# Two attention layers on one core: transposing and scaling the first half of the output inside the attention stage

## Chip, cores and metric

The kernel runs on one core of a Trainium2 chip. The metric is the device time of one execution in microseconds (us). PE is TensorE, DVE is VectorE, ACT is ScalarE, POOL is GpSimd and SP is SyncE, which here only issues DMAs.

## What is computed

The input is 1024 tokens of width 512. Four blocks follow each other, each with a residual and a layer norm: causal attention with 32 heads of width 16 and an adapter, a lookup feed-forward, causal attention with 32 query heads on 8 key/value heads, and a SwiGLU feed-forward. The change lies where an attention ends and its output projection begins:

```python
attn = jax.nn.softmax(scores, axis=-1)
y = jnp.einsum('bhqk,bhkd->bhqd', attn, v)
...
y = y + jnp.einsum('bhqk,xhkd->bhqd', ascores, av)     # first layer only
y = y.transpose(0, 2, 1, 3).reshape(B, T, C)
return jnp.einsum('btc,oc->bto', y, w_proj)
...
x = _layernorm(x + attention(x), axis=-1)
```

## The kernel before

The kernel is a series of stages. A stage is a block in which each engine runs its own list of instructions in order, held back only by semaphores, and all engines meet at its end. Two functions matter here, and each runs once for each layer.

`attention` works through 16 units. A unit is one group of four heads (`g`, eight groups) and one half of the tokens (`c`, 512 queries), in the order g0c0, g0c1, g1c0, and so on, so unit 15, the last, is a long one (c = 1, eight key tiles) and unit 14 is the last of the first token half. For each key tile PE makes the scores (L880), ACT takes their exponential (L969), POOL clears what lies above the diagonal (L1085), and PE multiplies with the values (`values`, L898) into PSUM bank 6. Each value row carries a column of ones, so a head gives 16 sums and one denominator, stored as 32 rows. When a unit is done ACT copies bank 6 to `o_raw` (`copy_o`, L976). Maxima are made ahead of the exponentials by PE into banks 4, 5 and 7 (L852) and reduced by DVE (L1034); in unit 15 nothing of that is left, and DVE has no work there. PE's list in unit 15 is four rounds (n = 0, 2, 4, 6) of two key tiles each: scores of later tiles, then the values of this round's two tiles.

`finish_attention` then takes the eight tiles of 128 tokens through a pipeline. In step s PE does up to four things, one after the other. In this text they have short names:

- T(s): eight transposes of `o_raw` into two PSUM banks (L1154). Banks 0 and 1 or 2 and 3 alternate. T(t) waits for the scaling of tile t - 2 for t of 2 and more.
- Y(s-1): four transposes of the scaled tile `y` into bank 4 (L1163). Y waits until ACT and DVE have taken the tile before from bank 4.
- Z(s-2): twelve matmuls with the output weights into bank 5 (L1173). Z waits for the split `y` of its tile and until DVE has added the tile before out of bank 5.
- X(s-4): four transposes of the normalised tile (L1182).

DVE scales a tile after T: a reciprocal of the denominators (L1221), a product (L1223) and in the first layer the sum with the adapter's part (L1227). After Y, ACT rounds (L1194) and DVE takes the rest (L1234). After Z, DVE adds the residual (L1246) and makes the layer norm (L1091, L1092, L1102, L1103), with a root on ACT (L1097).

Of the kernel before, what the change touches and what calls it, by code (L numbers as in the profile page):

```python
# [29 lines left out]
ALU = mybir.AluOpType  # L30
# [3 lines left out]
P = 128  # L34
T, C = 1024, 512
H, D = 32, 16
NT = T // P
# [72 lines left out]
def build(nc, d, out):  # L110
    with ExitStack() as stack:
# [5 lines left out]
        def at(name, offset, shape, dtype=F32):  # L117
# [83 lines left out]
        adapter(nc, d, ad, x_loaded, x_tok, v_tok, wv0_hl, x0_hl, arena_o, ident, gating, psum, stacked,  # L201
                wo[0], wo_hl[0])
        attention(nc, 0, att, stacked, arena_o, arena_p, arena_x, v_tok, v_grp, ident_b, maskb, psum,
                  (x_tok[:, :, :], d["x"].rearrange("(t p) c -> p t c", p=P), x_loaded), ad, ident)
        w1_raw = view(v_tok[:, :, :].rearrange("p t c -> p (t c)"), 0, [KC, C + 2 * P])
        finish_attention(nc, 0, d, x_loaded, x_tok, xT, ad["y"], arena_o, arena_s, w1_raw, wo[1],
                         wo_hl[0], yT_hl, ident, eps, psum, None, None)
# [9 lines left out]
            w_hl=w1_hl, x_hl=x1_hl, q_parts=q_parts[1], k_parts=k_parts[1], ones=ones, eps=eps,  # L217
            small_loads=[]))
        ff = SwigluArrays(nc, at)
        attention(nc, 1, att, stacked, arena_o, arena_p, arena_x, v_tok, v_grp, ident_b, maskb, psum)  # L220
        finish_attention(nc, 1, d, None, x_tok, xT, None, arena_o, arena_s, None, None, wo_hl[1],
                         yT_hl, ident, eps, psum, x2_hl, ff)
        swiglu(nc, d, x_tok, x2_hl, ff, s_gate, s_up, s_down, ones, eps, psum, out)
# [497 lines left out]
        self.load_k(sp, 0, 1)  # L721


def attention(nc, layer, phase, stacked, arena_o, arena_p, arena_x, v_tok, v_grp, ident_b, maskb,
              psum, x_load=None, ad=None, ident=None):

# [6 lines left out]
    pr = [view(a, 4096 * n, [2, 512]) for a in (arena_p, arena_x) for n in range(NP_RING // 2)]  # L733
    o_raw = view(arena_o, 0, [NG, T])
    vw = kr * D

    n_tiles = [4 * (c + 1) for c in range(CH)]
    steps = [(c, g) for g in range(NG) for c in range(CH)]
# [50 lines left out]
    with phase as ph, ExitStack() as own:  # L789
# [8 lines left out]
        scores_ready, exp_ready = ph.sem("scores_ready"), ph.sem("exp_ready")  # L798
        masked, pv_done = ph.sem("masked"), ph.sem("pv_done")
        o_copied, vg_ready = ph.sem("o_copied"), ph.sem("vg_ready")  # L800
        if ad:
            turn_ready, turn_taken, y_ready, y_copied = (ph.sem(n) for n in
                                                         ("turn_ready", "turn_taken", "y_ready", "y_copied"))
# [28 lines left out]
        def _(pe):  # L832
# [51 lines left out]
            def values(u, kt):  # L884
# [16 lines left out]
                                     start=kt == 0, stop=kt == 4 * c + 3, tile_position=(0, 32 * r))  # L901
                last.then_inc(pv_done, 2)

            issued = 0

            def maxima(u, slot):
                nonlocal issued
                while issued < issued_by(u, slot):
                    b = next(x for x in range(NU + 1) if issued < first_entry[x + 1])
                    entry(issued, b, lists[b][issued - first_entry[b]])  # L910
                    issued += 1
# [33 lines left out]
            for u, (c, _) in enumerate(steps):  # L945
                at = blocks.index((u, 0))
                for n in range(0, n_tiles[c], 2):
                    ahead = blocks[at + n + 2:at + n + 4]
                    for k, (au, akt) in enumerate(ahead):
                        for p in range(2 - k):  # L950
                            scores(au, akt, p)
                            maxima(u, 4 * n + 2 * (2 * k + p) + 1)
                    values(u, n)
                    values(u, n + 1)
                    maxima(u, 4 * n + 6)
                    if ahead:
                        scores(*ahead[1], 1)
                    maxima(u, 4 * n + 8)

        @block.scalar  # L960
        def _(act):
# [42 lines left out]
        @block.vector  # L1004
        def _(dve):
            def join_max(u):

                dve.wait_ge(qk_taken, first_entry[u] + len(lists[u]))
                dve.tensor_tensor(mx[:, u % 2, 0, :], mx[:, u % 2, 0, :], mx[:, u % 2, 1, :], ALU.max)\
                    .then_inc(max_joined, 1)  # L1010

            for b in range(NU + 1):
                if b == NU:
                    join_max(b - 1)
                for n, what in enumerate(lists[b]):
# [12 lines left out]
                    if n == 0 and b >= 2:  # L1028
                        dve.wait_ge(max_ready, b - 1)
                    src = psum[:, bank, 0:width * len(heads)]  # L1030
                    if len(heads) > 1:
                        src = src.rearrange("p (h k) -> p h k", h=len(heads))
                    col = 4 * heads[0] + i
                    dve.tensor_reduce(mx[:, b % 2, kc, col:col + 4 * len(heads) - 3:4], src, AX, ALU.max)\  # L1034
                        .then_inc(qk_taken, 1)

        @block.gpsimd
        def _(pool):
# [67 lines left out]
def finish_attention(nc, layer, d, x_loaded, x_tok, xT, y_ad, arena_o, arena_s, w_next, wo_next,  # L1106
# [5 lines left out]

    o_raw = view(arena_o, 0, [NG, T])
    y = view(arena_s, 0, [2, C])
    h = view(arena_s, 8192, [2, C])
    rec = view(arena_s, 12288, [H])
    stats = view(arena_s, 12416, [2, 9])
    with Phase(nc, f"fin{layer}") as ph:
# [27 lines left out]
        @block.tensor  # L1146
        def _(pe):
            for s in range(NT + 4):
                if s < NT:
                    t = s  # L1150
                    if t >= 2:
                        pe.wait_ge(y_ready, t - 1)
                    for g in range(NG):
                        last = pe.transpose(psum[:, 2 * (t % 2) + g // 4, P * (g % 4):P * (g % 4) + P],  # L1154
                                            o_raw[:, g, P * t:P * t + P], ident[:, :])
                    last.then_inc(oT_ready, 1)
                if 0 <= s - 1 < NT:
                    t = s - 1
                    pe.wait_ge(y_ready, t + 1)
                    if t >= 1:  # L1160
                        pe.wait_ge(yT_cut, t)
                    for k in range(KC):
                        last = pe.transpose(psum[:, 4, P * k:P * k + P],  # L1163
                                            y[:, t % 2, P * k:P * k + P], ident[:, :])
                    last.then_inc(yT_ready, 1)
                if 0 <= s - 2 < NT:
                    t = s - 2
                    pe.wait_ge(yT_cut, t + 1)
                    if t >= 1:
                        pe.wait_ge(z_added, t)  # L1170
                    for k in range(KC):
                        for n, (i, j) in enumerate(((0, 0), (0, 1), (1, 0))):
                            last = pe.matmul(psum[:, 5, :], yT_hl[i][:, t % 2, k, :], w_out[j][:, k, :],  # L1173
                                             start=k + n == 0, stop=k == KC - 1 and n == 2)
                    last.then_inc(z_ready, 1)
                if 0 <= s - 4 < NT:
# [33 lines left out]
        def _(dve):  # L1210
            link = Chain(dve, chain_s)
            for s in range(NT + 5):
                if s < NT:
                    t = s
                    dve.wait_ge(oT_ready, t + 1)
                    if t >= 2:
                        dve.wait_ge(yT_ready, t - 1)
                    o = psum[:, 2 * (t % 2):2 * (t % 2) + 2, :].rearrange("p b (h f) -> p (b h) f", f=VW)
                    if t >= 1:
                        dve.wait_ge(y_ready, t)  # L1220
# [17 lines left out]
                if 0 <= s - 2 < NT:  # L1238
                    t = s - 2
                    dve.wait_ge(z_ready, t + 1)  # L1240
                    dve.wait_ge(y_ready, t + 1)
# [608 lines left out]
```

## Time and profile before

| | |
|---|---|
| median of 3 runs | 990.2 us (989.58 to 993.11) |
| profiled execution, its own time | 991.25 us |
| span of that execution | 989.5 us |
| PE busy | 904.1 us (91%) |
| DVE busy | 650.1 us (66%) |
| ACT busy | 520.1 us (53%) |
| mean granted clock of TensorE | 0.951 |

Busy shares are means over stages with different limits; what a change in one stage is worth is read from that stage. The first attention stage ends at 388.5 us of the span, and the first finishing stage runs from 389.9 to 433.8 us. The second attention stage ends at 807.1 us, and the second finishing stage runs from 808.2 to 852 us.

### The profile page before, as it was taken

The page shows a single profiled execution, that of the slowest core. Times are in us where ns is not written, and L with a number is a line of the kernel's source. Part 1 is how long each engine was busy: PE and PEld are TensorE (multiplying, and loading weights), DVE is VectorE, ACT ScalarE, POOL GpSimd, SP SyncE. Part 2 cuts the span into 40 slices and gives each one's busy share as a digit, 9 for nine tenths or more (in the row PEclk, how much of TensorE's full clock was granted, in tenths as well). Part 3 has the DMA queues.
Part 4 walks back from the last instruction along what each step waited for, and adds up shares of the span by engine and source line. Part 5 has one row for each costly group of instructions (what it writes and reads, how often), then busy time and mean ns, then how long its engine had stood idle before and what let it go on. Part 6 is the DMA issues. An engine that isn't in the chain of part 4 may idle for free. (4 is left out here: it accounts for less than half of the span.)

```text
span 989.5 us, 15152 instructions
## 1 busy us (share of the span) xinstructions
PE 904.1 (91%) x5334; PEld 505.7 (51%) x5334; DVE 650.1 (66%) x1151; ACT 520.1 (53%) x1160; POOL 287.4 (29%) x527
## 2 busy tenths in 40 slices
PE   6897989999999997988698899999999889799997
PEld 4574864444344433845276234434344238577766
DVE  5953577878778841956745877887778418455464
ACT  4441236767677665224625066767777642367630
POOL 2675042322222321042346123322222230024200
PEclk9987999999999989997799689999999999899999
DMA  9333131211221202100024311101100010422001
GB/s 323 102 113 93 35 89 42 65 49 52 53 61 49 77 12 69 39 1 1 1 81 129 96 37 28 41 26 38 38 26 3 2 43 1 157 66 82 3 32 54
DMA packets 50029, 57.14 MB, mean 58 GB/s; under 512 B 8928, under 2 KB 39712, under 8 KB 49952
## 3 DMA queue, kind: packets, MB, share of 16 engines
q1 hardware_dynamic: 48320, 55.75, 18.9%
q8 instruction: 45, 0.74, 0.3%
q10 hardware_dynamic: 1632, 0.39, 0.2%
q14 instruction: 32, 0.26, 0.1%
HBM read 43.41 MB, written 12.32 MB: 56 GB/s over the span
## 5 line engine op out<-in xcount | busy, mean ns | idle before, releaser
L1034 DVE TENSOR_REDUCE mx<-psum 128x1 f32<-128x512 f32 (+3 forms) x640 | 371.2, 632 | 104.8 <-PE psum L857 59.5
L852 PE MATMUL psum<-arena_s 96*128 96x512 bf16 (+3 forms) x768 | 218.5, 338 | 10.9 <-PEq L247 5.3
L969 ACT ACTIVATE arena_p<-psum 128x512 f32<-128x512 f32 (+1 forms) x384 | 185.0, 591 | 68.3 <-PE psum L880 65.3
L880 PE MATMUL psum<-arena_s 99*128 99x512 bf16 (+3 forms) x768 | 203.0, 331 | 9.3 <-ACT arena_p L969 3.6
L969 ACT ACTIVATE arena_x<-psum 128x128 f32<-128x128 f32 (+2 forms) x384 | 133.9, 439 | 86.3 <-PE psum L880 63.4
L852 PEld LDWEIGHTS psum<-arena_s 96*128 96x128 bf16 x768 | 70.6, 98 | 116.4 <-DVE mx L1034 61.5
L880 PEld LDWEIGHTS psum<-arena_s 99*128 99x128 bf16 x768 | 66.6, 98 | 100.2 <-ACT arena_p L969 34.5
L1085 POOL TENSOR_SCALAR_AFFINE_SELECT arena_p<-arena_p 128x256 f32<-128x256 f32 x128 | 50.9, 408 | 203.5 <-ACT arena_p L969 203.5
L262 PE MATMUL psum<-x_h,w 128*128 128x512 f32 x224 | 88.1, 457 | 11.1 <-DVE w L500 7.9
L857 PE MATMUL psum<-maskb,ident_b 128*128 128x128 bf16 (+1 forms) x384 | 93.8, 244 | 0.0
L898 PE MATMUL psum<-arena_p,v_grp 128*32 128x512 f32 (+1 forms) x768 | 90.1, 589 | 0.0
L1085 POOL TENSOR_SCALAR_AFFINE_SELECT arena_x<-arena_x 128x256 f32<-128x256 f32 x128 | 51.4, 408 | 74.7 <-ACT arena_x L969 45.2
L898 PE MATMUL psum<-arena_x,v_grp 128*32 128x256 f32 (+2 forms) x768 | 59.3, 423 | 4.6 <-POOL arena_x L1085 4.6
L262 PEld LDWEIGHTS psum<-x_h,w 128*128 128x128 f32 x224 | 45.3, 202 | 27.6 <-DVE w L500 9.5
L1636 PE MATMUL psum<-x_h,ff_w 128*128 128x512 f32 (+1 forms) x176 | 45.7, 403 | 1.7 <-ACT ff_flags L1693 0.9
L563 POOL TENSOR_TENSOR arena_o<-arena_o 128x512 f32<-128x512 f32 x26 | 36.0, 1386 | 36.8 <-DVE arena_o L520 30.3
L262 PE MATMUL psum<-x_l,w 128*128 128x512 f32 x112 | 46.5, 416 | 0.0
L1173 PE MATMUL psum<-wo_h,yT 128*128 128x512 f32 x128 | 43.8, 403 | 1.6 <-DVE arena_s L1246 1.6
L1636 PE MATMUL psum<-x_l,ff_w 128*128 128x512 f32 (+1 forms) x176 | 45.2, 399 | 0.0
L898 PEld LDWEIGHTS psum<-arena_p,v_grp 128*32 128x32 f32 x768 | 20.6, 112 | 44.1 <-issue 29.2
L1656 PE MATMUL psum<-ff_wd,ff_g 128*128 128x512 f32 (+1 forms) x176 | 41.5, 396 | 1.6 <-ACT ff_wd L1689 1.6
L857 PEld LDWEIGHTS psum<-maskb,ident_b 128*128 128x128 bf16 x384 | 38.4, 100 | 7.5
(212 smaller groups left out, 1190.6 us busy)
## 6 DMA issues: line engine op xcount, KB each, us to landing
arena_s<-q_parts SPq DMA_DIRECT2D x32, 192.0 KB, 2.9
arena_s<-k_parts SPq DMA_DIRECT2D x96, 64.0 KB, 2.2
ff_raw<-in_w_in SPq DMA_DIRECT2D x11, 512.0 KB, 3.5
arena_s<-q_parts SPq DMA_DIRECT2D x32, 128.0 KB, 2.9
arena_w<-in_w SPq DMA_DIRECT2D x12, 256.0 KB, 6.5
q_parts<-arena_p SPq DMA_DIRECT2D x24, 128.0 KB
ff_wd_raw<-in_w_down SPq DMA_DIRECT2D x1, 2560.0 KB, 11.4
k_parts<-arena_p SPq DMA_DIRECT2D x18, 128.0 KB
```

Source lines behind the costliest of these rows:

```text
L262: last = pe.matmul(out, lhs[i](k), rhs[j](k), start=k + n == 0, stop=k == KC - 1 and n == 2)
L563: pool.tensor_tensor(rotated(n), t_cos[:, s, :], t_sin[:, s, :], ALU.add)\
L852: last = pe.matmul(psum[:, bank, width * n:width * n + width], q_st[0:KS, b % NS, 512 * r + P * i:512 * r + P * i + P], k_st[0:KS, g % NK, ...
L857: last = pe.matmul(psum[:, bank, 0:width * n].rearrange("p (h k) -> p h k", h=n) [:, :, width - P:width], ident_b[:, :], maskb[:, :].rearr ...
L880: pe.matmul(psum[:, 2 * (n % 2) + t, o:512], k_st[0:KM, g % NK, at:at + P], q_st[0:KM, u % NS, 512 * r + o:512 * r + 512], start=True, sto ...
L898: last = pe.matmul(psum[32 * r:32 * r + VW, 6, o:512], v_grp[:, u // CH % 2, kt, r if layer == 0 else 0, :], pr[(n + r // 2) % NP_RING][:, ...
L969: act.activation(pr[n % NP_RING][:, t, o:512], psum[:, 2 * (n % 2) + t, o:512], ACT.Exp, scale=scale).then_inc(exp_ready, 1)
L1034: dve.tensor_reduce(mx[:, b % 2, kc, col:col + 4 * len(heads) - 3:4], src, AX, ALU.max)\
L1085: pool.affine_select(out=tri, in_=tri, compare_op=ALU.is_ge, fill=0.0, base=0, pattern=[[0, 2], [1, P]], channel_multiplier=-1).then_inc(m ...
L1173: last = pe.matmul(psum[:, 5, :], yT_hl[i][:, t % 2, k, :], w_out[j][:, k, :], start=k + n == 0, stop=k == KC - 1 and n == 2)
L1636: last = pe.matmul(psum[0:rows[i], 2 * (n % 3) + u, :], ff.w_hl[a][:, i % 2, col:col + rows[i]], x_hl[b][:, k, 512 * c:512 * c + 512], sta ...
L1656: return pe.matmul(psum[:, 4 + t % 2, :], ff.g_hl[a][0:rows[i], i, P * t:P * t + P], ff.wd_hl[b][0:rows[i], i, :], start=(a, b, i) == (0, ...
```

## The change

T and the scaling of tiles 0 to 3 leave `finish_attention` and go into `attention`. These four tiles are the first token half, whose last unit (14) is copied to `o_raw` during unit 15. PE does T(0) after round 2 of unit 15, T(1) after round 4, and T(2) and T(3) after round 6, the last. All four use one pair of PSUM banks, 4 and 5, so T(t) waits for the scaling of tile t - 1 (`y_done`), where the finishing stage had two pairs. The scaled tiles go to an array of their own, `y_first`, from which Y(0) to Y(3) read in the finishing stage. There T and the scaling begin with tile 4, in step 4, as before.

```diff
+FIRST = 4
+def first_outputs(arena_s):
+    return view(arena_s, 24576, [FIRST, C]), view(arena_s, 32768, [H])
...
+    finish_after = {2: (0,), 4: (1,), 6: (2, 3)}
...
+            def turn_output(t):
+                if t == 0:
+                    pe.wait_ge(o_copied, NU - 1)
+                    pe.wait_ge(qk_taken, len(reached))
+                else:
+                    pe.wait_ge(y_done, t)
+                for g in range(NG):
+                    last = pe.transpose(psum[:, 4 + g // 4, P * (g % 4):P * (g % 4) + P],
+                                        o_raw[:, g, P * t:P * t + P], ident[:, :])
+                last.then_inc(oT_ready, 1)
...
                     maxima(u, 4 * n + 8)
+                    for t in finish_after.get(n, ()) if u == NU - 1 else ():
+                        turn_output(t)
...
+            for t in range(FIRST):
+                dve.wait_ge(oT_ready, t + 1)
+                if t:
+                    dve.wait_ge(y_done, t)
+                o = psum[:, 4:6, :].rearrange("p b (h f) -> p (b h) f", f=VW)
+                dve.reciprocal(rec, o[:, :, D]).then_inc(rec_done, 1)
...
+                scaled = dve.tensor_tensor(y_first[:, t, :].rearrange("p (h f) -> p h f", f=D), o[:, :, 0:D],
+                                           rec.rearrange("p (h o) -> p h o", o=1).broadcast_to([P, H, D]), ALU.mult)
+                if ad:
...
+                    scaled = dve.tensor_tensor(y_first[:, t, :], y_first[:, t, :], ad["y"][:, t, :], ALU.add)
+                scaled.then_inc(y_done, 1)
...
             for s in range(NT + 4):
-                if s < NT:
+                if FIRST <= s < NT:
                     t = s
-                    if t >= 2:
-                        pe.wait_ge(y_ready, t - 1)
+                    if t >= FIRST + 2:
+                        pe.wait_ge(y_ready, t - FIRST - 1)
...
+                    src = y[:, t % 2, :] if t >= FIRST else y_first[:, t, :]
```

These are PE's instructions in the first layer before the change, from round 2 of unit 15 to the first matmuls of the finishing stage (`arena_o` holds `o_raw`, `arena_s` operands and `y`, `arena_p` and `arena_x` the exponentials, and `yT` the split transposed tile).

```order
L898 MATMUL psum<-arena_x,v_grp 32x512 x8
L880 MATMUL psum<-arena_s 128x384 x2
L880 MATMUL psum<-arena_s 128x256 x4
L880 MATMUL psum<-arena_s 128x128 x2
L898 MATMUL psum<-arena_p,v_grp 32x512 x4
L898 MATMUL psum<-arena_p,v_grp 32x384 x4
L880 MATMUL psum<-arena_s 128x128 x2
L898 MATMUL psum<-arena_x,v_grp 32x256 x4
L898 MATMUL psum<-arena_x,v_grp 32x128 x4
L1154 MATMUL psum<-ident,arena_o 128x128 x16
L1163 MATMUL psum<-ident,arena_s 128x128 x4
L1154 MATMUL psum<-ident,arena_o 128x128 x8
```

After the last values (L898) the stage ended, and the next began with T(0) and T(1), Y(0) and T(2). This is the same place of PE's list in the changed kernel, where L880 is now L892, L898 is L910, T in the attention is L924, Y is L1206 and Z is L1215.

```order
L892 MATMUL psum<-arena_s 128x384 x2
L924 MATMUL psum<-ident,arena_o 128x128 x8
L892 MATMUL psum<-arena_s 128x256 x4
L892 MATMUL psum<-arena_s 128x128 x2
L910 MATMUL psum<-arena_p,v_grp 32x512 x4
L910 MATMUL psum<-arena_p,v_grp 32x384 x4
L892 MATMUL psum<-arena_s 128x128 x2
L924 MATMUL psum<-ident,arena_o 128x128 x8
L910 MATMUL psum<-arena_x,v_grp 32x256 x4
L910 MATMUL psum<-arena_x,v_grp 32x128 x4
L924 MATMUL psum<-ident,arena_o 128x128 x16
L1206 MATMUL psum<-ident,arena_s 128x128 x8
```

T(0) now stands ahead of the scores of the last two key tiles, T(1) ahead of the last values, and T(2) and T(3) behind them; the finishing stage begins with Y(0) and Y(1).

On DVE in the first layer the attention stage ended before with the maxima (L1034, L1009, L1025), and the scaling of tiles 0 and 1 opened the finishing stage.

```order
L1009 TENSOR_TENSOR mx<-mx 128x16
L1025 COPY mT<-psum 48x128
L247 UNCONDITIONAL_BRANCH
L1209 UNCONDITIONAL_BRANCH
L1221 RECIPROCAL arena_s<-psum 128x32
L1223 TENSOR_TENSOR arena_s<-psum,arena_s 128x512
L1227 TENSOR_TENSOR arena_s<-arena_s,arena_w 128x512
L1221 RECIPROCAL arena_s<-psum 128x32
```

In the changed kernel the scaling (L1067, L1069, L1074) stands ahead of the branch that ends the stage, four times; the last of the four and what follows read:

```order
L1067 RECIPROCAL arena_s<-psum 128x32
L1069 TENSOR_TENSOR arena_s<-psum,arena_s 128x512
L1074 TENSOR_TENSOR arena_s<-arena_s,arena_w 128x512
L248 UNCONDITIONAL_BRANCH
L1251 UNCONDITIONAL_BRANCH
L1276 TENSOR_TENSOR yT_78<-psum,yT_77 128x512 x2
L1289 TENSOR_TENSOR arena_s<-psum,x_tok 128x512
```

So the stage ends on DVE behind the fourth scaling, and the finishing stage starts on DVE with the rest of tiles 0 and 1 (L1276).

## Rows read from the trace of the kernel before

**Rows 1.** Windows: us; busy us (instructions) of PE, PEld, DVE, ACT, POOL; PEclk; DMA

```profile
373.80:388.50 14.70, 11.96 (x86) 3.35 (x85) 0.00 (x0) 10.76 (x27) 3.22 (x8) 1.00 0.01 2
...
389.90:433.80 43.90, 39.42 (x224) 33.01 (x224) 35.25 (x72) 11.73 (x25) 0.00 (x0) 0.96 0.17 61
404.80:418.40 13.60, 13.60 (x88) 11.89 (x85) 13.08 (x28) 3.28 (x8) 0.00 (x0) 1.00 0.01 1
```

**Rows 2.** Timeline of PE, end of the first attention stage: start us, us, instruction

```profile
382.42 0.72 PE L880 MATMUL psum<-arena_s 99*128 99x384 bf16 x4
...
384.49 1.71 PE L898 MATMUL psum<-arena_p,v_grp 128*32 128x512 f32 x16
386.13 0.29 PE L880 MATMUL psum<-arena_s 99*128 99x128 bf16 x2
386.35 0.64 PE L898 MATMUL psum<-arena_x,v_grp 128*32 128x256 f32 x8
387.44 0.42 PE L898 MATMUL psum<-arena_x,v_grp 128*32 128x128 f32 x8 [0.45 <-POOL arena_x L1085]
```

**Rows 3.** Timeline of ACT in the same stretch

```profile
383.61 1.56 ACT L969 ACTIVATE arena_x<-psum 128x256 f32<-128x256 f32 x6
...
387.93 0.59 ACT L976 COPY arena_o<-psum 128x512 f32<-128x512 f32 x1 [1.02 <-PE psum L898]
```

**Rows 4.** Timeline of all engines, start of the first finishing stage

```profile
389.90 3.55 PE L1154 MATMUL psum<-ident,arena_o 128*128 128x128 f32 x16 [2.04 <-PEq L250]
...
391.78 0.36 DVE L1221 RECIPROCAL arena_s<-psum 128x32 f32<-128x32 f32 x1 [27.17 <-PE psum L1154]
...
393.64 0.66 PE L1163 MATMUL psum<-ident,arena_s 128*128 128x128 f32 x4 [0.19 <-DVE arena_s L1227]
...
396.63 0.48 PE L1173 MATMUL psum<-wo_h,yT 128*128 128x512 f32 x1
...
400.70 0.48 PE L1173 MATMUL psum<-wo_h,yT 128*128 128x512 f32 x1
```

**Rows 5.** Timeline of all engines, from attention to finishing in the second layer

```profile
804.73 0.29 PE L880 MATMUL psum<-arena_s 99*128 99x128 bf16 x2
...
806.52 0.59 ACT L976 COPY arena_o<-psum 128x512 f32<-128x512 f32 x1 [1.02 <-PE psum L898]
...
808.17 1.94 PE L1154 MATMUL psum<-ident,arena_o 128*128 128x128 f32 x16 [1.72 <-PEq L250]
809.27 0.36 DVE L1221 RECIPROCAL arena_s<-psum 128x32 f32<-128x32 f32 x1 [27.77 <-PE psum L1154]
...
810.41 0.66 PE L1163 MATMUL psum<-ident,arena_s 128*128 128x128 f32 x4 [0.30 <-DVE arena_s L1223]
...
812.95 0.48 PE L1173 MATMUL psum<-wo_h,yT 128*128 128x512 f32 x1
...
817.00 0.48 PE L1173 MATMUL psum<-wo_h,yT 128*128 128x512 f32 x1
```

**Rows 6.** Timeline, first finishing stage: Z(6), its residual sum, and Z(7)

```profile
422.58 0.47 PE L1173 MATMUL psum<-wo_h,yT 128*128 128x512 f32 x1
...
425.61 0.69 DVE L1246 TENSOR_TENSOR arena_s<-psum,x_tok 128x512 f32<-128x512 f32 x1 [0.21 <-PE psum L1173]
...
426.45 0.47 PE L1173 MATMUL psum<-wo_h,yT 128*128 128x512 f32 x1 [0.44 <-DVE arena_s L1246]
```

**Rows 7.** Windows around the starts of stages, for the granted clock

```profile
387.90:389.90 2.00, 0.00 (x0) 0.03 (x1) 0.00 (x0) 0.59 (x1) 0.00 (x0) 1.00 0.00 0
390.00:393.00 3.00, 3.00 (x15) 3.00 (x16) 1.15 (x3) 0.00 (x0) 0.00 (x0) 0.50 0.67 170
393.50:394.00 0.50, 0.36 (x3) 0.36 (x4) 0.39 (x2) 0.00 (x0) 0.00 (x0) 1.00 1.03 418
...
808.20:812.00 3.80, 3.44 (x28) 2.96 (x28) 2.37 (x5) 0.59 (x1) 0.35 (x1) 1.00 0.69 249
...
851.00:857.00 6.00, 3.53 (x10) 2.81 (x11) 0.78 (x3) 1.98 (x3) 0.00 (x0) 0.50 0.55 192
```

More of the change, by code:

```diff
@@ L203, in build @@
         attention(nc, 0, att, stacked, arena_o, arena_p, arena_x, v_tok, v_grp, ident_b, maskb, psum,
-                  (x_tok[:, :, :], d["x"].rearrange("(t p) c -> p t c", p=P), x_loaded), ad, ident)
+                  arena_s, ident, (x_tok[:, :, :], d["x"].rearrange("(t p) c -> p t c", p=P), x_loaded), ad)
         w1_raw = view(v_tok[:, :, :].rearrange("p t c -> p (t c)"), 0, [KC, C + 2 * P])
@@ L219, in build @@
         ff = SwigluArrays(nc, at)
-        attention(nc, 1, att, stacked, arena_o, arena_p, arena_x, v_tok, v_grp, ident_b, maskb, psum)
+        attention(nc, 1, att, stacked, arena_o, arena_p, arena_x, v_tok, v_grp, ident_b, maskb, psum,
+                  arena_s, ident)
         finish_attention(nc, 1, d, None, x_tok, xT, None, arena_o, arena_s, None, None, wo_hl[1],
@@ L721, in load_first @@
         self.load_k(sp, 0, 1)
+FIRST = 4
+def first_outputs(arena_s):
+    return view(arena_s, 24576, [FIRST, C]), view(arena_s, 32768, [H])
 def attention(nc, layer, phase, stacked, arena_o, arena_p, arena_x, v_tok, v_grp, ident_b, maskb,
[L725 removed]
+              psum, arena_s, ident, x_load=None, ad=None):
     q_st, k_st, q_loaded, k_loaded, kr = stacked.q, stacked.k, stacked.q_loaded, stacked.k_loaded, stacked.kr
@@ L735, in attention @@
     vw = kr * D
+    y_first, rec = first_outputs(arena_s)
+    finish_after = {2: (0,), 4: (1,), 6: (2, 3)}
     n_tiles = [4 * (c + 1) for c in range(CH)]
@@ L800, in attention @@
         o_copied, vg_ready = ph.sem("o_copied"), ph.sem("vg_ready")
+        oT_ready, y_done, rec_done = ph.sem("oT_ready"), ph.sem("y_done"), ph.sem("rec_done")
         if ad:
@@ L1035, in _ @@
                         .then_inc(qk_taken, 1)
+            for t in range(FIRST):
[4 more added lines that the diff above has]
+                dve.reciprocal(rec, o[:, :, D]).then_inc(rec_done, 1)
+                dve.wait_ge(rec_done, (2 if ad else 1) * t + 1)
+                scaled = dve.tensor_tensor(y_first[:, t, :].rearrange("p (h f) -> p h f", f=D), o[:, :, 0:D],
+                                           rec.rearrange("p (h o) -> p h o", o=1).broadcast_to([P, H, D]), ALU.mult)
+                if ad:
+                    scaled.then_inc(rec_done, 1)
+                    dve.wait_ge(rec_done, 2 * t + 2)
+                    scaled = dve.tensor_tensor(y_first[:, t, :], y_first[:, t, :], ad["y"][:, t, :], ALU.add)
+                scaled.then_inc(y_done, 1)
         @block.gpsimd
@@ L1114, in finish_attention @@
     y = view(arena_s, 0, [2, C])
+    y_first, _ = first_outputs(arena_s)
     h = view(arena_s, 8192, [2, C])
@@ L1158, in _ @@
                     t = s - 1
-                    pe.wait_ge(y_ready, t + 1)
+                    if t >= FIRST:
+                        pe.wait_ge(y_ready, t - FIRST + 1)
                     if t >= 1:
                         pe.wait_ge(yT_cut, t)
+                    src = y[:, t % 2, :] if t >= FIRST else y_first[:, t, :]
                     for k in range(KC):
-                        last = pe.transpose(psum[:, 4, P * k:P * k + P],
-                                            y[:, t % 2, P * k:P * k + P], ident[:, :])
+                        last = pe.transpose(psum[:, 4, P * k:P * k + P], src[:, P * k:P * k + P], ident[:, :])
                     last.then_inc(yT_ready, 1)
@@ L1212, in _ @@
             for s in range(NT + 5):
-                if s < NT:
+                if FIRST <= s < NT:
                     t = s
-                    dve.wait_ge(oT_ready, t + 1)
-                    if t >= 2:
+                    dve.wait_ge(oT_ready, t - FIRST + 1)
+                    if t >= FIRST + 2:
                         dve.wait_ge(yT_ready, t - 1)
                     o = psum[:, 2 * (t % 2):2 * (t % 2) + 2, :].rearrange("p b (h f) -> p (b h) f", f=VW)
-                    if t >= 1:
-                        dve.wait_ge(y_ready, t)
+                    if t > FIRST:
+                        dve.wait_ge(y_ready, t - FIRST)
                     link(dve.reciprocal(rec, o[:, :, D]))
@@ L1240, in _ @@
                     dve.wait_ge(z_ready, t + 1)
-                    dve.wait_ge(y_ready, t + 1)
+                    if t >= FIRST:
+                        dve.wait_ge(y_ready, t - FIRST + 1)
                     if t >= 2:
```

## The prediction

> **What bounds the kernel now.** I read the page first for the shares of the engines, then windows around the places that the change touches, and then the timeline there, since everything hangs on the order of a few instructions. The last unit of the attention is shared by PE and ACT: from 373.8 to 388.5 us PE is busy 11.96 of 14.70 us and ACT 10.76, while DVE does nothing [rows 1]. That idle DVE is where the moved scaling can go. The finishing stage is the opposite: in its full steps, 404.8 to 418.4 us, PE is busy all of 13.60 us and DVE 13.08 [rows 1]. Work taken out of these steps would come out of the time. But the four tiles that leave are those of steps 0 to 3, and from step 4 on every step has the same work as before. So what the finishing stage can give back is only the time from its first instruction to Z(1), which is step 3. I therefore look at two stretches in each layer: how much later the attention stage ends, and how much sooner Z(1) comes after the start of the next.
>
> **What the finishing stage gives back.** In the first layer it runs from T(0) at 389.90 to Z(1) at 400.70, 10.80 us [rows 4]; in the second from 808.17 to 817.00, 8.83 us [rows 5]. After the change it opens with Y(0). From Y(0) to Z(0) the second layer shows 810.41 to 812.95, 2.54 us, with the round through ACT and DVE that stays [rows 5]; DVE was busy with other tiles there, so this is not too little. From Z(0) to Z(1) nothing is left between but the residual sum out of bank 5, which Z(1) must wait for. Z(6) to Z(7) is such a step: 422.58 to 426.45, 3.87 us, in which PE waited for that sum [rows 6]. Together 6.41 us. The gain is 10.80 - 6.41 = **4.4 us in the first layer** and 8.83 - 6.41 = **2.4 us in the second**, at full clock. It is not the sum of the removed work (four times eight transposes and their scalings): T(2) and T(3) lay largely beside the residual sum of the bank before, and without them PE waits for DVE instead.
>
> **What the attention stage takes.** T(0) goes in front of four score matmuls on which ACT waits next. PE had issued L880 with 384 columns at 382.42 and went on at once, and ACT began the next exponentials at 383.61 [rows 2, 3]. Sixteen transposes at full clock are busy 1.94 us [rows 5], so T(0) costs PE some 0.95 us, of which ACT's backlog covers about half; I take 0.4 us (bounds 0 and 0.95). The scores at 386.13 [rows 2] then come at 386.5, and T(1) starts at about 386.7. T(1) delays the last values by another 0.2 to 0.5 us, since PE waited 0.45 us for POOL's mask there [rows 2]. The values alone would end 0.7 us later, and so would ACT's copy, which ended at 387.93 + 0.59 = 388.52 [rows 3].
>
> But the stage no longer ends with that copy. T(1), T(2) and T(3) share one pair of banks, so they form a chain: transposes, scaling, transposes, and so on. One link at full clock: transposes to the first DVE instruction 808.17 to 809.27, 1.10 us [rows 5]; scaling until PE's next instruction that waited for it 391.78 to 393.64, 1.86 us in the first layer [rows 4], and 809.27 to 810.41, 1.14 us in the second, which has no sum with the adapter [rows 5]. A link is 2.96 us or 2.24 us.
>
> First layer: T(1) at 386.7, three links, end of the last scaling at 386.7 + 3 x 2.96 = 395.6, less 0.06 for the last hand-over to PE: 395.5. The stage ended at 388.52, so it ends **7.0 us later**. Second layer: the same scores stand at 804.73 and ACT's copy ended at 806.52 + 0.59 = 807.11 [rows 5]. T(1) at 805.3, three links of 2.24 give 812.0: **4.9 us later**. ACT's copy of unit 15 and the last values lie hidden under this chain, so their own delay costs nothing. Semaphores, barrier and branch between the stages stay (1.38 us from 388.52 to PE's first transpose [rows 3, 4], 1.06 us in the second layer [rows 5]); three more semaphores I cost at nothing, beside that. Behind the barrier the first layer's weight loads on SP start later by as much; the lookup stage that reads them is over 40 us away, so they stay hidden [rows 1].
>
> Net at full clock: 7.0 - 4.4 = +2.6 us and 4.9 - 2.4 = +2.5 us, together **+5.1 us**.
>
> **The clock.** In the tail PE works about 1 us of each link and waits the rest, then waits for the barrier, does Y(0), and waits for ACT and DVE again. What such gaps do is in the trace: PE stood still from 387.9 to 389.9, and from 390 the granted clock is 0.50, the 1.2 GHz level, until shortly before 393.5, where it is 1.00 again [rows 7]. Before the SwiGLU stage, with PE busy 3.53 of 6 us, it is 0.50 for 851 to 857 us [rows 7]. The second finishing stage kept 1.00 over a gap of 1.7 us [rows 5, 7], so one gap does not always do it; five in a row, as here, nearly always should. The old low stretch in the first layer fell on T(0) and T(1) and is in the 10.80 us already. The new one falls on T(3), Y(0) and the first part of Z(0). T(3): eight transposes to DVE take 1.88 instead of 1.10 us (389.90 to 391.78 against rows 5) [rows 4, 5], 0.8 us. Y(0), half as many: 0.4 us. Z(0) takes 422.58 to 425.61, 3.0 us, from its first matmul to the sum [rows 6], of which some 2.7 us go with the clock; at half clock throughout it would cost 2.7 us more. I take a third, 0.9 us, since PE is then busy and the clock came back within about 3.5 us before. That is 2.1 us for each layer, bounds 0 and 5.0 (T(2), T(3), Y(0), Y(1) and all of Z(0): 0.8 + 0.8 + 0.4 + 0.4 + 2.7). Both layers: **+4.3 us**.
>
> The sum is 5.1 + 4.3 = +9.4 us. On the profiled execution's own time, 991.25 us (its span of 989.5 and 1.75 around it), this gives 1000.6. That execution is 1.05 us above the median of the runs, so the forecast for the median is 990.2 + 9.4 = **999.6 us**.
>
> **Rivals.**
> 1. *The clock stays up*, as it did at the start of the second finishing stage [rows 7]. Then +5.1 us: 995.3. Against it: more and longer waits of PE than there. 0.19.
> 2. *The clock stays down longer*: all transposes from T(2) and all of Z(0) at 1.2 GHz, 5.0 us for each layer, so 5.1 + 10.0 = +15.1: 1005.3. It would be so if transposes did not raise the clock. The trace speaks against it: from 389.9 to 393.5 PE did nothing but transposes (T(0), T(1), then Y(0) at 393.64) and the clock came back [rows 4, 7]. Still two low stretches in a row can happen, as from 851 to 857 [rows 7]. 0.17. The Trainium skill has a rule that would make this the rule and not the exception ("TensorE: Matmul & The Clock Gate", Part 4: PE-mode transpose): the full clock doesn't engage for transposes, which don't count as busy in the same way. By that rule the forecast would be near 1005; this trace disagrees, by the clock of 1.00 at 393.5 after transposes alone.
> 3. *The moved work hides*, which would be faster. If all four scalings were done before the last values end, the attention stages would end only 0.7 us later each, and 4.4 + 2.4 would be gained: 1.4 - 6.8 = -5.4 us, 984.8. T(0) starts near 382.8 and the values would end at 389.2, so four links have to fit into 6.4 us: it decides when a link takes 1.6 us or less. The shortest in the trace is 2.24 us [rows 5]. 0.04.
> 4. *The chain costs less than counted*, for instance as T(1) starts sooner or later steps of the finishing stage gain too, now that DVE enters step 4 with no arrears (DVE was busy 13.08 of 13.60 us there [rows 1]). Half a microsecond in each of the four steps with T left, in both layers, is 4 us: 5.1 - 4 = +1.1, 991.3. Against it: PE is just as full there. 0.08.
>
> **How the numbers follow.** The likeliest case, chain and one low stretch in each layer, has 0.52. A measurement of this kernel can tell about 0.5% (5 us) from no change, so within 0.5% means up to 995.2. That is rival 4 and half of rival 1, and a little of the likeliest: 0.19. Faster is rival 3 alone with a little for what I don't see: 0.05. Slower by over 0.5%: 0.76. The range reaches from just under rival 1 to rival 2: 994.3 to 1005.5. It leaves out rivals 3 and 4 and the far end of rival 2, no more than 0.2.
>
> **What the profile of the changed kernel would show.** The attention stage should end on DVE with L1069 or L1074, some 7 us (first layer) and 5 us (second) after the point where ACT's copy ended before, relative to the start of unit 15. L1067 should start four times, the last three 3.0 us apart in the first layer and 2.2 in the second, and waits for PE of about 1.1 us ahead of each. PE should wait for DVE ahead of T(2) and T(3) (L924), nearly 2 us and over 1 us. From the finishing stage's first PE instruction to Z(1) there should be 6.4 us, more by what the clock takes. Granted clock: 0.5 somewhere between the last values and Z(0). From step 4 on the steps should be as long as before. The prediction is wrong if T(2) starts right behind the last values without a wait, if the finishing stages shorten by more than 5 and 3 us, or if the time is won or lost outside these two places.

## Result and profile after

The changed kernel took 1004.93 us (median of 4 runs, 999.65 to 1007.76) against 991.65 us (median of 4, 989.58 to 994.66). The ratio estimated from these runs is 1.0128, 95% interval 1.0094 to 1.0162 (the two medians alone give 1.0134). In a second comparison it was 1.0105 (1.0078 to 1.0132). So the change makes the kernel slower by about 1 to 1.3%, 10 to 13 us. The forecast was 999.6 us.

| profiled execution | before | after |
|---|---|---|
| own time | 991.25 us | 1004.54 us |
| span | 989.5 us | 1002.8 us |
| PE busy | 904.1 us | 911.0 us |
| DVE busy | 650.1 us | 650.2 us |
| mean granted clock | 0.951 | 0.938 |

DVE does the same work as before. PE is busy 7 us more with the same number of matmuls, 5334: it ran longer at the lower clock.

The timeline of PE in the changed kernel, from the values of round 2 of unit 15 in the first layer to Z(1); it answers to [rows 2] and [rows 4] (start us, us, instruction, idle time before it and what ended it):

```profile
381.15 1.92 PE L910 MATMUL psum<-arena_x,v_grp 128*32 128x512 f32 x16
383.00 0.50 PE L892 MATMUL psum<-arena_s 99*128 99x384 bf16 x2
383.34 1.04 PE L924 MATMUL psum<-ident,arena_o 128*128 128x128 f32 x8
...
387.10 0.28 PE L892 MATMUL psum<-arena_s 99*128 99x128 bf16 x2
387.23 1.04 PE L924 MATMUL psum<-ident,arena_o 128*128 128x128 f32 x8
388.20 0.86 PE L910 MATMUL psum<-arena_x,v_grp 128*32 128x256 f32 x16
390.17 1.09 PE L924 MATMUL psum<-ident,arena_o 128*128 128x128 f32 x8 [1.11 <-DVE arena_s L1074]
393.17 1.19 PE L924 MATMUL psum<-ident,arena_o 128*128 128x128 f32 x8 [1.90 <-DVE arena_s L1074]
397.63 1.09 PE L1206 MATMUL psum<-ident,arena_s 128*128 128x128 f32 x4 [3.28 <-PEq L251]
400.12 1.11 PE L1206 MATMUL psum<-ident,arena_s 128*128 128x128 f32 x4 [1.40 <-DVE yT L1276]
400.89 0.77 PE L1215 MATMUL psum<-wo_h,yT 128*128 128x512 f32 x1
...
406.33 0.47 PE L1215 MATMUL psum<-wo_h,yT 128*128 128x512 f32 x1 [0.44 <-DVE arena_s L1289]
```

T(0) and T(1) stand in the stream without a wait. T(2) and T(3) each waited for the scaling of the tile before, 1.11 and 1.90 us, and the next stage begins only at 397.63. DVE and ACT at the same place; ACT's copy answers to [rows 3]:

```profile
388.31 0.36 DVE L1067 RECIPROCAL arena_s<-psum 128x32 f32<-128x32 f32 x1 [2.05 <-PE psum L924]
...
391.30 0.36 DVE L1067 RECIPROCAL arena_s<-psum 128x32 f32<-128x32 f32 x1 [1.19 <-PE psum L924]
...
394.39 0.36 DVE L1067 RECIPROCAL arena_s<-psum 128x32 f32<-128x32 f32 x1 [1.28 <-PE psum L924]
...
395.51 0.69 DVE L1074 TENSOR_TENSOR arena_s<-arena_s,arena_w 128x512 f32<-128x512 f32 x1
```

```profile
389.12 0.58 ACT L1002 COPY arena_o<-psum 128x512 f32<-128x512 f32 x1 [1.25 <-PE psum L910]
```

The copy that used to end the stage is done at 389.70; the last scaling is done at 396.20. The second layer shows the same with shorter links (PE):

```profile
812.36 0.28 PE L892 MATMUL psum<-arena_s 99*128 99x128 bf16 x2
...
814.71 1.09 PE L924 MATMUL psum<-ident,arena_o 128*128 128x128 f32 x8 [0.39 <-DVE arena_s L1069]
816.98 1.09 PE L924 MATMUL psum<-ident,arena_o 128*128 128x128 f32 x8 [1.18 <-DVE arena_s L1069]
820.30 0.73 PE L1206 MATMUL psum<-ident,arena_s 128*128 128x128 f32 x4 [2.23 <-PEq L251]
822.42 1.11 PE L1206 MATMUL psum<-ident,arena_s 128*128 128x128 f32 x4 [1.40 <-DVE yT L1276]
823.19 0.78 PE L1215 MATMUL psum<-wo_h,yT 128*128 128x512 f32 x1
...
829.08 0.47 PE L1215 MATMUL psum<-wo_h,yT 128*128 128x512 f32 x1 [0.44 <-DVE arena_s L1289]
```

The windows for the clock, as in [rows 7] (busy us of PE, PEld, DVE, ACT, POOL; granted clock; DMA):

```profile
391.50:393.00 1.50, 0.00 (x0) 0.00 (x0) 1.43 (x3) 0.00 (x0) 0.00 (x0) 1.00 0.00 0
394.50:397.50 3.00, 0.00 (x0) 0.00 (x0) 1.63 (x3) 0.00 (x0) 0.00 (x0) 0.50 0.00 0
397.50:404.00 6.50, 4.97 (x15) 3.94 (x16) 1.38 (x2) 2.46 (x3) 0.00 (x0) 0.50 0.83 287
404.50:406.50 2.00, 1.56 (x10) 1.14 (x9) 0.98 (x2) 0.00 (x0) 0.00 (x0) 1.00 0.77 281
814.00:820.50 6.50, 2.70 (x30) 1.99 (x23) 2.75 (x5) 0.58 (x1) 0.00 (x0) 1.00 0.00 0
821.00:827.50 6.50, 5.10 (x15) 4.21 (x15) 1.38 (x2) 2.46 (x3) 2.17 (x2) 0.50 0.47 164
```

In both layers the 1.2 GHz level (0.50) covers Y(1) and nearly all of Z(0), and in the first Y(0) too.

**Where the time went.** I measure each layer from the start of the values of round 2 to the start of Z(1), the first point from which both kernels do the same again. First layer: 380.56 to 400.70 before, 20.14 us (the row of 380.56 is in the fence below; Z(1) in [rows 4]); 381.15 to 406.33 after, 25.18 us: **+5.04**. Second layer: 799.16 to 817.00 [rows 5], 17.84 us; 806.41 to 829.08, 22.67 us: **+4.83**. Together +9.9 of the +13.3 us between these two executions. The two rows of before, and the one of after in the second layer:

```profile
380.56 1.92 PE L898 MATMUL psum<-arena_x,v_grp 128*32 128x512 f32 x16
...
799.16 1.92 PE L898 MATMUL psum<-arena_x,v_grp 128*32 128x512 f32 x16
```

```profile
806.41 1.92 PE L910 MATMUL psum<-arena_x,v_grp 128*32 128x512 f32 x16
```

The other 3.4 us lie outside the two stretches: 0.6 us before round 2 of unit 15 of the first layer (380.56 to 381.15), 1.6 us from Z(1) of the first layer to round 2 of unit 15 of the second, 1.2 us behind Z(1) of the second. Behind Z(1) the finishing stage itself runs as before: Z(1) to Z(7) took 25.75 us before and 25.71 after in the first layer, 26.01 and 26.03 in the second. The runs of one and the same kernel differ by more than 3.4 us (984.01 to 995.61 us in 23 runs of the kernel before). The same holds for this part alone: span less the two stretches is 951.5 us before and 955.0 in both profiles of the changed kernel, but 956.3 us in the kernel before with filler (see the experiments), which does the same work there. So the 3.4 us are within its scatter.

One such piece can be seen in the kernel before, in round 0 of unit 15 of the second layer, which the change doesn't touch. Its values took 3.62 us, and 1.92 us in the two-tile kernel (the second line, from "two tiles again"):

```profile
792.73 3.62 PE L898 MATMUL psum<-arena_p,v_grp 128*32 128x512 f32 x16
```

```profile
796.61 1.92 PE L910 MATMUL psum<-arena_p,v_grp 128*32 128x512 f32 x16
```

The granted clock of the stretch around the first was 0.80 (790.67 to 799.16 us); in the first layer, from 373.80 to 380.56, it was 1.00.

### The profile page after: what moved, and what is told of

Its sections match the earlier page's. It is cut to its first block and busy times, and to the rows that moved or that the text cites. A ratio compares the mean times of both kernels' runs of the same rounds, so it can differ in the third digit from the quotient of the medians.

```text
span 1002.8 us, 15143 instructions
## 1 busy us (share of the span) xinstructions
PE 911.0 (91%) x5334; PEld 509.7 (51%) x5334; DVE 650.2 (65%) x1151; ACT 520.6 (52%) x1160; POOL 287.0 (29%) x527
## 5 line engine op out<-in xcount | busy, mean ns | idle before, releaser
L892 PE MATMUL psum<-arena_s 99*128 99x512 bf16 (+3 forms) x768 | 203.9, 335 | 8.0 <-ACT arena_p L995 2.9
L892 PEld LDWEIGHTS psum<-arena_s 99*128 99x128 bf16 x768 | 66.9, 98 | 98.6 <-ACT arena_p L995 32.4
L910 PE MATMUL psum<-arena_p,v_grp 128*32 128x512 f32 (+1 forms) x768 | 90.0, 588 | 0.0
L910 PE MATMUL psum<-arena_x,v_grp 128*32 128x256 f32 (+2 forms) x768 | 58.9, 422 | 3.7 <-POOL arena_x L1125 3.7
L1215 PE MATMUL psum<-wo_h,yT 128*128 128x512 f32 x128 | 46.4, 425 | 2.5 <-DVE arena_s L1289 2.5
L910 PEld LDWEIGHTS psum<-arena_p,v_grp 128*32 128x32 f32 x768 | 20.6, 112 | 44.4 <-issue 29.9
```

What stands on the lines that cost most here:

```text
L892: pe.matmul(psum[:, 2 * (n % 2) + t, o:512], k_st[0:KM, g % NK, at:at + P], q_st[0:KM, u % NS, 512 * r + o:512 * r + 512], start=True, sto ...
L910: last = pe.matmul(psum[32 * r:32 * r + VW, 6, o:512], v_grp[:, u // CH % 2, kt, r if layer == 0 else 0, :], pr[(n + r // 2) % NP_RING][:, ...
```

## Experiments

All edits are against the changed kernel unless said otherwise. The ratio of each run is to runs of the kernel before that were timed beside it. "Two stretches" is the sum over both layers of the time from the values of round 2 to Z(1) in the profiled execution; it was 37.98 us before and 47.85 us in the changed kernel.

| run | ratio to before (95% interval) | two stretches, against before |
|---|---|---|
| changed kernel | 1.0128 (1.0094 to 1.0162) | +9.9 us |
| changed kernel again | 1.0105 (1.0078 to 1.0132) | +11.0 us |
| first layer only | 1.0056 (1.0032 to 1.0079) | +6.5 us |
| second layer only | 1.0039 (1.0016 to 1.0061) | +4.6 us |
| more banks | 1.0069 (1.0044 to 1.0093) | +5.2 us |
| filler | 1.0057 (1.0034 to 1.0080) | +6.3 us |
| two tiles | 0.9957 (0.9931 to 0.9984) | -4.0 us |
| two tiles again | 0.9923 (0.9902 to 0.9944) | -4.0 us |
| two tiles early | 0.9962 (0.9942 to 0.9981) | see there |
| two tiles, filled | 0.9923 (0.9895 to 0.9951) | -4.6 us |
| two tiles, filled, again | 0.9952 (0.9933 to 0.9971) | -4.5 us |
| before, filled | 1.0017 (1.0001 to 1.0033) | 0.0 us |

**Two tiles only.**

```diff
-FIRST = 4
+FIRST = 2
...
-    finish_after = {2: (0,), 4: (1,), 6: (2, 3)}
+    finish_after = {2: (0,), 4: (1,)}
```

> Only T(0) and T(1) with their scalings move into the attention stage (rounds 2 and 4 of unit 15); T(2) and T(3) stay in the finishing stage. Theory, the chain through one pair of banks: the loss is the two links behind the last values, which are gone here. The scaling of tile 1 ended 1.0 us (first layer) and less than 0.6 us (second) after the old end of the stage; the finishing stage keeps nearly all of its gain, 4.2 and 2.2 us at full clock, since T(2) fits into the wait between Y(0) and Y(1). Net about -4.8 us against the kernel before, -3 to -6 with a low clock here or there. Rival, the moved transposes and scalings themselves cost the time (PE and DVE work in the middle of the scores): half of the work moved, half of the loss, +6 us.

0.9957, 4.3 us less than before, and 0.9923 (7.6 us less) when it was run again; the two stretches gave 4.0 us in both profiles, where 4.8 were forecast. The rival's +6 us is out. The kernel is faster with half of the move and slower with all of it. DVE in the first layer, then ACT:

```profile
386.40 0.69 DVE L1074 TENSOR_TENSOR arena_s<-arena_s,arena_w 128x512 f32<-128x512 f32 x1
...
390.73 0.36 DVE L1263 RECIPROCAL arena_s<-psum 128x32 f32<-128x32 f32 x1 [0.23 <-PE psum L1195]
```

```profile
386.10 0.59 ACT L1002 COPY arena_o<-psum 128x512 f32<-128x512 f32 x1 [1.25 <-PE psum L910]
```

The last scaling of the stage is done at 387.09, 0.4 us behind ACT's copy (386.69): the moved work hides but for about 1 us. Counted from the values of round 2, the finishing stage starts 10.40 and 9.66 us later, before 9.34 and 9.01 us. And T(2), now in the finishing stage, costs nothing there, since it stands between Y(0) and Y(1), where PE waited 1.40 us in the changed kernel. Y(0) to Y(1) took 2.03 us with T(2) between them, and the same 2.03 us in the filler run below, without T(2) and at full clock:

```profile
388.52 0.63 PE L1206 MATMUL psum<-ident,arena_s 128*128 128x128 f32 x4 [2.49 <-PEq L251]
388.99 1.70 PE L1195 MATMUL psum<-ident,arena_o 128*128 128x128 f32 x8
390.55 1.11 PE L1206 MATMUL psum<-ident,arena_s 128*128 128x128 f32 x4
```

**Two tiles, one round earlier.**

```diff
-FIRST = 4
+FIRST = 2
...
-    finish_after = {2: (0,), 4: (1,), 6: (2, 3)}
+    finish_after = {0: (0,), 2: (1,)}
```

> The same two tiles, one round earlier each (rounds 0 and 2 of unit 15). Theory of the chain: the scaling of tile 1 ends some 4 us sooner, well before ACT's last copy, so the stage ends with that copy, later only by what the transposes cost PE in the stream, 0.4 us each: +0.8 instead of +1.0 in the first layer, nearly the same in the second. So within 1 us of the run with rounds 2 and 4. Rival, transposes ahead of scores cost more the earlier they stand, since ACT waits for PE through the whole unit: 1 us or more slower than the run with rounds 2 and 4.

0.9962 beside 0.9957 in the same comparison, with medians of 988.70 and 986.26 us. The two intervals overlap for the most part, so the times neither show that the two kernels are within 1 us nor exclude the rival's 1 us or more. The profiles bear out the chain for the attention stage. T(0) stands here ahead of the values of round 2, so I measure from ACT's copy of unit 14 to the first instruction of the finishing stage: 16.85 and 16.53 us (373.73 to 390.58, 791.06 to 807.59), and 17.17 and 16.42 us in "two tiles again" (376.94 to 394.11, 794.58 to 811.00). To Z(1) it is 24.26 and 23.86 us, against 24.55 and 22.92: 0.65 us more in sum, all of it in the second finishing stage, where the clock was low this time (Y(0) took 1.08 us instead of 0.63). The kernel before took 26.90 and 26.33 us, but 1.7 us of the second figure are the low stretch in round 0 shown above.

**More banks.**

```diff
-                else:
+                elif t == 1:
                     pe.wait_ge(y_done, t)
+                else:
+                    pe.wait_ge(exp_ready, 2 * first_exp[NU])
                 for g in range(NG):
-                    last = pe.transpose(psum[:, 4 + g // 4, P * (g % 4):P * (g % 4) + P],
+                    last = pe.transpose(psum[:, (4, 4, 0, 2)[t] + g // 4, P * (g % 4):P * (g % 4) + P],
...
-                o = psum[:, 4:6, :].rearrange("p b (h f) -> p (b h) f", f=VW)
+                bank = (4, 4, 0, 2)[t]
+                o = psum[:, bank:bank + 2, :].rearrange("p b (h f) -> p (b h) f", f=VW)
```

> All four tiles moved as in the changed kernel, but T(2) writes banks 0 and 1 and T(3) banks 2 and 3, which are free after the last exponential, so that both start right behind the last values and wait for no scaling. Theory of the chain: behind tile 1 only the scalings follow one another (1.8 us in the first layer, 1.1 in the second) and no transposes stand between them: each layer's attention stage ends some 2.3 us sooner than in the changed kernel, -4.6 us in all, and still 2 to 5 us slower than before. Rival, the barrier or what lies behind it sets the loss: no difference to the changed kernel (0 us).

1.0069, between before and the changed kernel. PE and then DVE in the first layer:

```profile
390.02 0.86 PE L910 MATMUL psum<-arena_x,v_grp 128*32 128x256 f32 x16
390.81 1.97 PE L926 MATMUL psum<-ident,arena_o 128*128 128x128 f32 x16
397.20 1.03 PE L1209 MATMUL psum<-ident,arena_s 128*128 128x128 f32 x4 [4.42 <-PEq L251]
```

```profile
392.04 0.36 DVE L1070 RECIPROCAL arena_s<-psum 128x32 f32<-128x32 f32 x1
...
393.96 0.36 DVE L1070 RECIPROCAL arena_s<-psum 128x32 f32<-128x32 f32 x1
```

T(2) and T(3) follow the last values at once, and the scalings 1.92 us apart instead of 3.09. From the values of round 2 (382.97) to the end of the last scaling (395.07 + 0.69) it is 12.8 us, in the changed kernel 15.05 (381.15 to 396.20): 2.3 us less, as forecast. In the second layer it is 11.2 (806.49 to 817.73, where the last product ends) against 12.78 (806.41 to 818.50 + 0.69): 1.5 us less where 2.3 were forecast, as DVE waited 0.73 us for T(2) there. DVE's scalings alone, three of 1.9 us in a row from 390.13 to 395.76, still end behind the copy (391.54). The whole was 6.8 us slower than before (4.4 to 9.2), so the forecast of 2 to 5 us was likely too low; its two stretches came to +5.2 us. PE had nothing to do for 4.42 us behind T(3), and the clock was low afterwards here too (Y(0) took 1.03 us).

**Filler.**

```diff
                 last.then_inc(oT_ready, 1)
+                for _ in range({2: 14, 3: 24}.get(t, 0) if ad else {2: 8, 3: 16}.get(t, 0)):
+                    pe.transpose(psum[:, 7, 0:P], ident[:, :], ident[:, :])
...
                     last.then_inc(yT_ready, 1)
+                    for _ in range(10 if t == 0 else 0):
+                        pe.transpose(psum[:, 7, 0:P], ident[:, :], ident[:, :])
```

> The changed kernel, with added transposes of the identity into PSUM bank 7, which nobody reads: 14 and 24 behind T(2) and T(3) in the first layer, 8 and 16 in the second, 10 behind Y(0) in both. They fill PE's waits with about 0.11 us each and should delay nothing. Theory: the low clock between T(3) and Z(0) cost 2.3 us in each layer; with PE busy the clock stays at its upper level and the time falls by up to 4.6 us against the changed kernel, at least 2. Rival, transposes don't hold the clock up: Z(0) runs at the lower level as before, and the time is the same or a few tenths longer.

1.0057. Windows over the end of the attention stage and the start of the finishing stage, first and second layer:

```profile
389.00:396.00 7.00, 6.33 (x54) 5.86 (x54) 3.48 (x6) 0.00 (x0) 0.00 (x0) 1.00 0.00 0
396.50:403.00 6.50, 5.56 (x34) 4.58 (x34) 1.77 (x3) 2.46 (x3) 0.00 (x0) 1.00 0.74 252
812.00:818.00 6.00, 4.97 (x48) 4.33 (x40) 2.59 (x5) 0.59 (x1) 0.00 (x0) 1.00 0.00 0
818.00:825.00 7.00, 5.57 (x34) 4.58 (x34) 2.12 (x4) 2.46 (x3) 2.66 (x2) 1.00 0.42 150
```

The clock stays at 1.00 throughout, though from 389.9 to 396 PE did transposes alone. Y(0) to Z(1) took 6.32 us in both layers (397.13 to 403.45, 818.74 to 825.06), 2.4 us less than the 8.70 and 8.78 us of the changed kernel. T(2) and T(3) start 3.0 and 2.3 us apart as without filler. But the expectation that the filler delays nothing failed behind T(3): the filler there ended at 395.71 and 817.66, the last scalings at 394.94 and 817.03, and the finishing stage began 17.15 and 14.49 us after the values of round 2, 0.7 and 0.6 us later than in the changed kernel (16.48 and 13.89). So the clock gave back 4.8 us and the filler took 1.3 of them: the two stretches fell from +9.9 to +6.3 us. The changed kernel was not timed beside this one; against its two ratios, 1.0128 and 1.0105, the time fell by 5 to 7 us.

**The changed kernel again.**

> The changed kernel once more, on the chip of the next three, so that its time rests on more than four runs. Two stages account for +9.9 us of the +13.3 us between the two profiled executions. Theory: the rest is scatter of the clock elsewhere, and the median over more runs lies nearer +10 than +13. Rival: something that I haven't seen costs 3 us each time, and the median stays at +13.

1.0105, which is 10.4 us, with a median of 1004.09 us beside 992.88 (11.2 us): nearer +10 than +13, but with only 6 runs the two intervals overlap, and a constant further cost of 2 us is not excluded. In this profile T(3) ran at the lower clock (1.97 us instead of 1.19), and its two stretches cost +11.0 us.

**One layer each.** The count of moved tiles becomes a number for each layer, `FIRSTS = (4, 0)` or `(0, 4)`, read in both functions.

> T(0) to T(3) and their scalings are moved in the first layer alone; the second is as before. From the profile of the changed kernel the two stages of the first layer cost +5.0 us. Theory: the layers add up, so +5 us against the kernel before. Rival, one layer carries it all through what follows it (the lookup stage and its loads on SP): +10 or 0.

> The move in the second layer alone. Its two stages cost +4.8 us in the profile of the changed kernel: +5 us against the kernel before, and with the run on the first layer the two add up to the whole. Rival as there: 0 or +10.

1.0056 and 1.0039, 5.6 and 3.9 us (by the medians 5.5 and 1.8 us). Their sum, 9.5 us, is near what the whole change cost in the same comparison, 10.4 us. The intervals, 3.2 to 7.8 and 1.6 to 6.1 us, exclude that one layer costs nothing or all of it, but they leave 1 or 2 us for each open. In the profiles the moved layer's stretch cost 5.5 and 4.7 us. The other 1.0 us of the +6.5 in the table lies in the second layer of the first run, whose stages are as before: after the same wait as in [rows 5] the clock fell there, and T(0) and T(1) took 2.95 us instead of 1.94:

```profile
814.24 2.95 PE L1197 MATMUL psum<-ident,arena_o 128*128 128x128 f32 x16 [1.75 <-PEq L251]
```

**Filler behind the last values.** With two tiles moved, and for comparison in the kernel before:

```diff
+            for _ in range(8):
+                pe.transpose(psum[:, 7, 0:P], ident[:, :], ident[:, :])
```

> Two tiles moved (rounds 2 and 4), plus 8 transposes of the identity into the unused bank 7 behind the last values, which fill some 0.9 us of the 2.5 us in which PE waited for the next stage. In the run without them the clock fell 3.3 us after PE's last values, and T(2), Y(1) and Z(0) of the first layer took about 1.5 us longer than at full clock. Theory: the wait gets shorter than what makes the clock fall, and up to 1.5 us are won against the run without filler. Rival: the wait of 1.6 us that is left is enough, and nothing changes, or 0.2 us are lost as the stage ends later.

> Two tiles moved with the 8 filling transposes, once more: -5.5 to -7.5 us against the kernel before, 1.5 to 3 us less than without the filler.

> Two tiles moved, no filler, once more and on the same chip as the two beside it: -4 us against the kernel before.

> The kernel before, with nothing moved, plus the 8 transposes of the identity behind the last values of each attention stage. It is the control for the run with two tiles and filler. Theory, the move and the filler give separate gains: the filler alone saves the low stretch at the start of the first finishing stage (about 1.7 us before) and nothing in the second, which had none in the profile, so -1 to -2 us. Rival, the filler gives the whole gain of that run and the move of two tiles little: -4 us or more.

With filler the two-tile kernel measured 0.9923 and 0.9952, without it 0.9957 and 0.9923. The order turned round between the two comparisons, so the filler is worth nothing that these runs can tell. My 1.5 to 3 us were wrong, and so were the -4 us for the second run without filler (it measured -7.6) and the -5.5 us or more for the second with it (-4.8). In the control the filler made the first finishing stage of the kernel before start at full clock, yet the time was 1.0017, 1.7 us more where I had expected 1 to 2 us less. Its profile, PE:

```profile
390.45 1.09 PE L961 MATMUL psum<-ident 128*128 128x128 f32 x8
392.92 1.94 PE L1157 MATMUL psum<-ident,arena_o 128*128 128x128 f32 x16 [1.38 <-PEq L251]
395.89 0.66 PE L1166 MATMUL psum<-ident,arena_s 128*128 128x128 f32 x4 [1.03 <-DVE arena_s L1230]
```

T(0) and T(1) take 1.94 us there instead of 3.55 [rows 4], but half of that was not on the path: Y(0) now waits 1.03 us for the scaling of tile 0 where it waited 0.19, and the stretch from T(0) to Z(1) is only 0.8 us shorter. Both finishing stages start 0.4 us later behind the filler, and the two stretches come out at 0.0 us (19.73 and 18.21 us). The rival, that the filler and not the move made the two-tile kernel fast, is refuted.

## Why the prediction was right

The direction and the mechanism were right, and the size was forecast too small: 999.6 us against 1004.93. Of the 5.3 us between them 1.45 are the reference, whose median moved from 990.2 us of 3 runs to 991.65 of 4; the other 3.9 are the loss, 13.3 us by the medians where 9.4 were forecast. The time lies only 0.6 us below the upper end of the range, 1005.5, and that end was set by a case, rival 2, to which I had given 0.17.

**The gain of the finishing stage** was forecast as 4.4 and 2.4 us, from a stretch of 6.41 us from Y(0) to Z(1) at full clock. The filler run showed 6.32 us in both layers. Right, and for the reason given: Z(1) waits for the residual sum (0.44 us of idle ended by L1289, as at Z(7) before). Rival 4, a gain in the later steps, is out by the unchanged time from Z(1) to Z(7). In the changed kernel itself the low clock ate most of this gain: from its first instruction to Z(1) the finishing stage took 8.70 and 8.78 us, before 10.80 and 8.83.

**The chain in the attention stage** was forecast to end 7.0 and 4.9 us later. Measured, with the shift of the round-2 values taken out: 396.20 - 388.52 - 0.59 = 7.1 us; and 819.19 - 807.11 - 7.25 = 4.8 us. The link was 2.99 us (388.31 to 391.30) where 2.96 was forecast. PE's wait ahead of T(3) was the forecast one, 1.90 and 1.18 us; ahead of T(2) it was shorter, 1.11 and 0.39 us, as the last values stand in that link. The way from the last scaling to PE's next instruction, 1.43 and 1.11 us, is that from ACT's copy before, 1.38 and 1.06. T(0) cost 0.4 us in the stream: from the values of round 2 to the last scores 5.57 us before and 5.95 us after. The more-banks run took the bank out of the chain, and the two-tile run took the tail out altogether; both moved the time as that part says. So the loss comes from the two links behind the last values, with the clock that fell there, and not from the moved work as such.

**The clock** was forecast at 2.1 us for each layer. It was 2.3 and 2.4 us (8.70 and 8.78 less 6.41). That the sum fits is in part luck, since two of its terms were off in opposite directions. T(3), forecast at 0.8 us, cost 0.1 us in the first layer and nothing in the second, as it still ran at full clock. Z(0), forecast at 0.9 us for a third of it, cost 1.6 and 2.0 us (400.89 to 405.49 and 823.19 to 828.24, where 3.03 us was its length at full clock): the low stretch, in the first layer 394.2 to 404.2 us, took nearly all of it. In the second profile T(3) had it as well. That the clock stays up when transposes fill the waits was shown by the filler run. The Trainium skill says that the full clock doesn't engage for transposes ("TensorE: Matmul & The Clock Gate", Part 4: PE-mode transpose); this run disagrees for the 128x128 f32 transposes of this kernel, by a granted clock of 1.00 from 389 to 396 us, in which PE did nothing else.

**The sum** was +9.4 us. The two places came to +9.9 us in the profile, the timed runs to +12.7 and +10.4 us. What lies outside the two places I had at 0, and it was 3.4 us in the first pair of profiles. By the letter of the prediction time lost there is a sign that it is wrong; the work there is the same, and the profiles of kernels with the same work there differ by as much. Whether some of it belongs to the change is open: the median of all 10 runs of the changed kernel is 1004.6 us, inside the range, but no run separates a constant 1 or 2 us from scatter.

**What I missed** is the nearest better kernel. I said that T(2) and T(3) lay largely beside the residual sum, so that moving them gains little, and that their two links cost most of the tail. From these two sentences it follows that moving two tiles is faster than before; the runs gave 0.9957 and 0.9923 for it.

## What to carry to other kernels

Work moved into an idle engine is free only as long as its chain, counted with every hand-over and every buffer that it must wait for, ends before what used to end the stage. Move as many pieces as fit and leave the rest: here two of four tiles gained 0.4 to 0.8%, all four lost 1.0 to 1.3%. And ask of each piece what it lay beside at its old place: T(2) and T(3) filled waits of PE, so that taking them out won next to nothing (at full clock Z(0) to Z(1) took 4.06 us with T(3) between them, in the second layer of the two-tile run, and 3.88 without, in the filler run). Count the waits that the move makes as well: here the clock fell in them.

## What the runs showed of the hardware

The granted clock fell in the changed kernel at about 394.2 us, in the middle of T(3), although PE had never stood still for longer than 1.90 us since the last values, which ended at 389.06. In the second profile of the same kernel it fell sooner, at about 391.7 us, between T(2) and T(3). With transposes in these waits it stayed at 1.00, over 7 us with PE busy 6.33 us, all of it with transposes.

The same wait does not always have the same effect. Between the stages of the second layer PE stood still for 1.72 us in the kernel before and the clock stayed at 1.00 [rows 5, 7]; in the run with the first layer only, where these stages are unchanged, it stood still for 1.75 us and the clock fell at about 815.0 us, 0.8 us into the transposes behind that wait, which made the stretch 1.0 us longer.

A low stretch avoided at one place need not show in the whole: the control with filler avoided the one at the start of the first finishing stage and was no faster (1.0017, 1.0001 to 1.0033).
